# Residuals and the norms' scale and shift in natural rows on VectorE, and the front of a conditioned transformer block as two streams, each shifted by itself

## The chip, the cores and the metric

The kernel runs on one core of a Trainium2 chip. A core has five engines with an instruction queue each: TensorE (PE, matmuls into PSUM), VectorE (DVE), ScalarE (ACT), GpSimd (POOL) and SyncE (SP, which here only issues DMAs). They meet through semaphores alone. The metric is the device time of one launch in microseconds (us); less is better.

## What is computed

For each of 32 samples b (256 rows of 256 numbers), cut to what matters:

```python
x = rotate(x, theta[b], phi[b])                              # groups of 4 columns
h = gelu(x @ Wi[e] + bi[e])                                  # e = expert of the sample, 256 -> 1024
x = layernorm(h @ Wo[e] + bo[e] + x) * gamma[e] + beta[e]    # residual, norm 1
c = branch of the sample                                     # 0 or 1: two products; 2: three, through 512
x = layernorm(x + branch_c(x)) * gamma2 + beta2              # residual, norm 2
scale, shift = split(silu(sin_emb(t[b])) @ W_ada + b_ada)    # two rows of 256
x = layernorm(x) * (1 + scale) + shift                       # norm 3
q, k, v = x @ Wq + bq, x @ Wk + bk, x @ Wv + bv              # 16 heads of 16
s = q @ k.T / 4 + bias[b, head];  s[mask] = -inf
x = x + softmax(s) @ v @ Wo + bo                             # residual
x = x + gated_gelu((layernorm(x) * g2 + beta2) @ W1 + b1) @ W2 + b2
```

## The kernel before, in words

**Precision and layouts.** A product of width 256 takes its operand turned (columns on partitions). The products behind the first norm use operands split in a high and a low part (`xa_hi`, `xa_lo` for the branch, `xb_hi`, `xb_lo` for q, k and v, `xc_hi`, `xc_lo` in the tail): three matmuls for one. Norms work in natural rows (rows of the sample on partitions), so each norm's result is turned by TensorE (`transposed`, 128x128 pieces against `ident`), and ScalarE copies it out of PSUM.

**Scale and shift.** Before the change, norm 1 and norm 3 are scaled and shifted after the turn, when gamma and beta are numbers per partition: `affine_T` on ScalarE does two ACTIVATEs from PSUM into `gelu_out` and one more for the high part. VectorE then makes the low part.

**Residuals.** They are added by TensorE into the PSUM bank that collects the product. `open_wide` opens `SUM_F` with the bias row and adds x through eight matmul instructions of `x0` against `ident`; `add_residual` adds `xa_hi` and `xa_lo` in the branch, and `xb_hi` and `xb_lo` in the tail (bank `SUM_T`), through four matmuls each against `eye`. The bias row is picked by a 128x128 selector; for norm 1 and the branch ScalarE fills it anew for each sample (`stage_sel`). In the tail ScalarE copies `SUM_T` to `xo_nat` before VectorE takes its statistics.

**Three streams.** `front(b)` holds the rotation, the wide expert product (four steps m2 = 0 to 3 of `wide_in`, gelu on ScalarE, `wide_out`), norm 1, the branch, norms 2 and 3, and q, k, v. `attention(b)` holds 16 heads: on TensorE `scores` into `pS` and `turn` into `pX`, on VectorE bias, row maximum and subtraction (two times L1106, two times L913), on ScalarE the exponential. `tail(b)` holds the output product and the feed-forward part. Each is a generator, one step at a `yield`.

**What sets the order.** `ORDER` has a string per engine; each letter takes the next step of f (front), h (attention) or r (tail). One pass over the string is a turn; in turn n an engine goes through `front(n)`, `attention(n - 1)` and `tail(n - 2)`:

```python
streams = {"f": front(it) if it < NB else None,
           "h": attention(it - 1) if it else None,
           "r": tail(it - 2) if it >= 2 else None}
for letter in ORDER[engine]:
```

A turn begins with the wide product. Its four steps use PSUM banks 0 and 1 in turn (`BANK`), and the branch, q, k and v share the same two. An engine never overtakes itself: a waiting instruction holds all that stands behind it in its queue.

**Start.** In the first turn the weights are loaded in eleven pieces and split (`w_hi` on ScalarE, `w_lo` on VectorE); `weights()` hands out one portion per step. Pieces 6 to 10 reuse staging space of earlier ones, so SyncE's queue waits for their split. ScalarE's functions lie in table sets: Gelu in one, Exp and Tanh in another, and a change of set is an instruction of its own (ACT_TABLE_LOAD).

Of the kernel before, what the change touches and what calls it, by code (L numbers as in the profile page):

```python
# [7 lines left out]
P = 128  # L8
F32 = mybir.dt.float32
# [9 lines left out]
VECTORS = (("L2_cond_b1_sr", 4), ("L2_cond_b2_sr", 2), ("L3_cond_b_ada", 4), ("L3_cond_bq", 2), ("L3_cond_bk", 2),  # L19
# [20 lines left out]
    "PE": "ffffhfhhfhhhhfrfhhrrhhfhhfhrhhffhrfhhrhhrhhrhhhhrhhfrhhffhhhrhhhfrhhfh",  # L40
    "ACT": "ffhfhfhrhrhfhfhrfrhrhrrhhrhhhfhrfrfhrhhfhfh",
    "DVE": "hhhhrfhfhrfrhfrhhfrfhrrhfhfrhhfrhffhrrhfrhhfhrf",
    "POOL": "frff",
    "SP": "hhhffhfhhfhhhhhhhhffhffhffr",
}


BANK = {"wide0": 0, "wide1": 1, "wide2": 0, "wide3": 1, "y1": 0, "narrow": 0, "deep0": 0, "deep1": 1, "deep2": 0,
        "x2": 1, "x0": 0, "q": 1, "k": 0, "v": 1}
# [4 lines left out]
    "dma_angles", "dma_ints", "dma_consts", "dma_idx", "dma_sels", "dma_rows", "dma_cols", "dma_bcast", "dma_ada",  # L54
# [4 lines left out]
    "dma_x", "dma_chosen", "dma_mask", "dma_out", "dma_spill", "dma_raw0", "dma_raw1", "dma_raw2", "dma_raw3", "dma_stack0",  # L59
    "dma_stack1", "dma_bias0", "dma_bias1", "dma_bias2", "dma_bias3",  # L60

    "dve_front", "x0_made", "x0_turned", "x0_copied", "sel_made", "wide_in", "wide_gelu", "wide_out",
    "y1_made", "y1_turned", "x1_aff", "x1_hi", "x1_lo", "pe_narrow", "act_narrow", "dve_narrow", "pe_deep", "act_deep",
    "dve_deep", "branch_done", "y2_scaled", "x2_made", "x2_turned", "x2_aff", "x2_hi", "x2_lo", "qkv", "qk_hi", "qk_lo",
# [4 lines left out]
    "dve_tail", "ctxT", "ctx_hi", "ctx_lo", "wo", "xo_made", "ffn_in_made", "ffn_turned", "x3_aff", "x3_hi", "x3_lo",  # L69
    "w1", "tanh", "gated", "ffn_hi", "ffn_lo", "w2", "out_made",  # L70

    "front_var", "front_eps", "front_rstd", "tail_var", "tail_eps", "tail_rstd")
# [10 lines left out]
def conditioned_stack(nc, x_in, fside_in, mask_in, a, out_d):  # L83
# [14 lines left out]
    with ctx:  # L98
# [6 lines left out]
        eye = sb("eye", [P, P], F32R)  # L105
# [36 lines left out]
        xb = [(sb(f"xb_hi{i}", [P, K, S], F32R), sb(f"xb_lo{i}", [P, K, S], F32R)) for i in range(2)]  # L142
# [3 lines left out]
        xo_nat = sb("xo_nat", [P, T, H])  # L146
        ffn_in = sb("ffn_in", [P, T, H])
        gamma2 = sb("gamma2", [P, H])
# [4 lines left out]
        chosen = sb("chosen", [P, 2, M + 2 * K + K])  # L153
        mod = sb("mod", [P, 2 * K, NB])
# [7 lines left out]
        bias_raw = xo_nat[0:NROWS, 0, :]  # L162

        bias_rows = sb("bias_rows", [P, H], F32R)
        select = sb("select", [R2, 2, NB])
        stage_sel = sb("stage_sel", [P, 2, P], F32R)

        sels = sb("sels", [P, 3 * P + NM], F32R)
        o_sel, ff_sel, v_sel = (sels[:, n * P:(n + 1) * P] for n in range(3))
        hid_sel = sels[:, 3 * P:3 * P + NM]  # L170
        zero_sel = sb("zero_sel", [P, P], F32R)
        ones = sb("ones", [R2, P])
        idx = sb("idx", [1, 3, NB], I32)
        stats, mean_var, var_eps, rstd = ({which: sb(f"{which}_{name}", [P, T] + size) for which in ("front", "tail")}
# [11 lines left out]
        q_spill = nc.dram_tensor("q_spill", (2, 2, 3, HD * NPAIR * S), F32, kind="Internal").ap()  # L186
        k_spill = nc.dram_tensor("k_spill", (2, 2, 3, HD * NPAIR * S), F32, kind="Internal").ap()
# [4 lines left out]
        sels_raw = flat(ctx_nat[:, :, :])[:, 3 * NB:3 * NB + 3 * P + NM]  # L192
# [3 lines left out]
        trig = xo_nat[:, 1, 0:6 * NB].rearrange("p (q n) -> p q n", q=2)  # L196
        emb_act = scratch[:, 9 * NB:11 * NB].rearrange("p (q n) -> p q n", q=2)
        ada = gated[:, :, :, :].rearrange("p a b c -> p (a b c)").rearrange("p (k n) -> p k n", k=K)
# [36 lines left out]
        def interleave(engine, front, attention, tail, weights=None):  # L235

            extra = weights() if weights else iter(())
            for it in range(NB + 2):
                streams = {"f": front(it) if it < NB else None,
                           "h": attention(it - 1) if it else None,  # L240
                           "r": tail(it - 2) if it >= 2 else None}
                for letter in ORDER[engine]:
                    if streams[letter] is not None:
                        next(extra, None)
                        next(streams[letter], None)
                assert all(s is None or next(s, "end") == "end" for s in streams.values())


        def sync_program(e):
# [19 lines left out]
            def load_chosen(b):  # L269

                if b >= 2:
                    e.wait_ge(sem["branch_done"], b - 1)
                n = M + 2 * K
                load(chosen[:, b % 2, 0:n], a["expert_cols"].rearrange("e p n -> p e n")
                     [:, bass.ds(chosen_expert[b], 1), :].rearrange("p a n -> p (a n)"), "dma_chosen")
                c = e.value_load(idx[0:1, 1, b:b + 1], min_val=0, max_val=2)
                load(chosen[:, b % 2, n:n + K], a["branch_cols"].rearrange("e p n -> p e n")
                     [:, bass.ds(c, 1), :].rearrange("p a n -> p (a n)"), "dma_chosen")

            def load_x(b):  # L280
                if b:
                    e.wait_ge(sem["x0_turned"], b)
                load(flat(x_nat[:, :, :]), x_in[b], "dma_x")
# [22 lines left out]
            fetch_expert(0, 3)  # L306

            def weights():
# [12 lines left out]
                load_x(1)  # L321
# [8 lines left out]
                for u in range(NBIAS):  # L330
                    load_bias(u)
                yield

            def front(b):
# [6 lines left out]
                if b + 2 < NB:  # L341
                    load_x(b + 2)
# [947 lines left out]
```

## Time and profile before

| | us |
|---|---|
| median of three runs (range) | 2272.45 (2271.24 to 2272.83) |
| the profiled execution, its own time | 2269.38 |
| its span, first to last instruction | 2267.6 |
| busy PE / DVE / ACT / POOL | 2071.2 / 1456.6 / 1213.6 / 141.5 |
| mean granted TensorE clock | 0.981 |

Busy time is a union of instructions on an engine. Matmuls overlap in the pipeline, so what one costs in a dense stretch is the distance from its start to the next start. Of the 32 samples, 10 take the branch with three products (52 high parts of branch activations are made: one for a sample of the short branches, three for one of the long).

### The profile page before, as it was taken

What the parts mean: (1) busy time and instruction counts of PE and PEld (TensorE: products, weight loads), DVE (VectorE), ACT (ScalarE), POOL (GpSimd) and SP (SyncE); (2) the same over time, 40 slices, a digit from 0 to 9 for tenths busy, and PEclk for the clock granted to TensorE, in tenths of its full rate; (3) what the DMA queues carried; (4) which work ended last, traced back from release to release, by engine and by line L of the source; (5) the groups of instructions that cost most, each with busy time, mean ns of one, the idle gap of its engine ahead of it and who ended that gap; (6) DMA issues with size and microseconds to landing.
All of it is one profiled execution on the core that took longest, in us unless ns stands there. A gap on an engine that the chain in (4) does not pass through costs nothing.

```text
span 2267.6 us, 44771 instructions
## 1 busy us (share of the span) xinstructions
PE 2071.2 (91%) x15545; PEld 1823.4 (80%) x15545; DVE 1456.6 (64%) x5093; ACT 1213.6 (54%) x2151; POOL 141.5 (6%) x269
## 2 busy tenths in 40 slices
PE   5789999999999999999999999999999999999976
PEld 4678888888888888888888878888888888888865
DVE  4456776666676566676666776666676666677653
ACT  3455555555555655555555555555555565555532
POOL 1000000000000000000000000000000000000000
PEclk8889999999999999999999999999999999999988
DMA  5554445555444554444554445554545555444440
GB/s 197 160 152 135 151 123 163 165 159 147 138 144 142 160 160 138 153 144 140 164 169 128 136 142 155 164 169 141 151 140 138 164 165 157 140 146 125 121 129 24
DMA packets 208341, 330.98 MB, mean 146 GB/s; under 512 B 27970, under 2 KB 114402, under 8 KB 208098
## 3 DMA queue, kind: packets, MB, share of 16 engines
q1 hardware_dynamic: 208098, 327.79, 49.2%
q8 instruction: 147, 2.41, 0.4%
q14 instruction: 96, 0.79, 0.1%
HBM read 268.99 MB, written 58.72 MB: 145 GB/s over the span
## 4 chain that ended last, share of the span: by engine, by line
PE 76%; DVE 14%; issue 5%; ACT 3%; DMA 0%; POOL 0%; SPq 0%; DVEq 0%; POOLq 0%; ACTq 0%
PE pD L388 48%; PE pX L614 10%; PE pS L388 9%; PE pC L388 6%; DVE x_scores L1106 4%; DVE x_scores L913 3%; PE pD L393 3%; DVE x_nat L910 2%; PE pC L634 1%; ACT L713 1%; DVE y_nat L910 1%; ACT gated L713 1%; DVE gated L916 1%; DVE y_nat L1002 1%; ACT probs L713 1%
## 5 line engine op out<-in xcount | busy, mean ns | idle before, releaser
L1106 DVE CUSTOM_DVE_ANT_0 x_scores<-pS,bias_ring 128x256 f32<-128x256 f32 x1024 | 391.5, 419 | 410.0 <-PE pS L388 407.6
L713 ACT ACTIVATE probs<-pX 128x512 f32<-128x512 f32 x512 | 305.1, 596 | 471.5 <-PE pX L614 469.2
L614 PE MATMUL pX<-ident,x_scores 128*128 128x128 f32 x2048 | 327.2, 283 | 107.5 <-DVE x_scores L913 69.5
L614 PEld LDWEIGHTS pX<-ident,x_scores 128*128 128x128 f32 x2048 | 226.1, 142 | 177.1 <-DVE x_scores L913 106.1
L913 DVE TENSOR_SCALAR x_scores<-x_scores,row_max 128x256 f32<-128x256 f32 x1024 | 315.5, 350 | 18.3
L388 PE MATMUL pS<-k_stack,q_stack 96*128 96x256 f32 x1024 | 304.7, 380 | 0.0
L713 ACT ACT_TABLE_LOAD x188 | 241.2, 1283 | 25.7 <-DVE xa_lo L910 21.9
L388 PE MATMUL pD<-raw,gelu_out 128*128 128x256 f32 x1024 | 241.8, 379 | 0.0
L388 PE MATMUL pD<-x,raw 128*128 128x256 f32 x1024 | 239.2, 382 | 1.0 <-ACT x L713 0.8
L388 PEld LDWEIGHTS pS<-k_stack,q_stack 96*128 96x128 f32 x1024 | 197.9, 193 | 22.3
L388 PEld LDWEIGHTS pD<-x,raw 128*128 128x128 f32 x1024 | 191.3, 192 | 25.5 <-issue 1.6
L388 PE MATMUL pD<-w_hi,ffn 128*128 128x256 f32 x1024 | 210.1, 288 | 0.6 <-ACT ffn L713 0.6
L388 PE MATMUL pS<-mask_add,eye_bf 128*128 128x512 bf16 x512 | 196.0, 383 | 10.6 <-issue 8.6
L388 PEld LDWEIGHTS pD<-raw,gelu_out 128*128 128x128 f32 x1024 | 184.9, 190 | 20.2
L713 ACT ACTIVATE gelu_out<-pD,chosen 128x256 f32<-128x256 f32 x364 | 158.1, 486 | 50.5 <-PE pD L388 36.2
L388 PEld LDWEIGHTS pD<-w_hi,ffn 128*128 128x128 f32 x1024 | 167.8, 191 | 14.0 <-issue 12.3
L713 ACT ACTIVATE gated<-pD 128x512 f32<-128x512 f32 x128 | 75.9, 593 | 149.1 <-PE pD L388 149.1
L1191 POOL TENSOR_SCALAR front_var_eps<-front_mean_var 128x2 f32<-128x2 f32 x96 | 29.7, 309 | 1860.9 <-DVE front_mean_var L995 1860.9
L388 PE MATMUL pC<-probs,v_aug 128*17 128x256 f32 x2048 | 139.4, 391 | 0.7 <-issue 0.7
L388 PE MATMUL pD<-xc_hi,w_hi 128*128 128x256 f32 x512 | 129.1, 284 | 0.0
L388 PE MATMUL pD<-xc_hi,w_lo 128*128 128x256 f32 x512 | 129.0, 284 | 0.0
L388 PE MATMUL pD<-w_lo,ffn 128*128 128x256 f32 x512 | 127.8, 282 | 0.0
(155 smaller groups left out, 3795.6 us busy)
## 6 DMA issues: line engine op xcount, KB each, us to landing
bias_ring<-in_fside SPq DMA_DIRECT2D x512, 256.0 KB, 2.7
raw<-in_experts SPq DMA_DIRECT2D x128, 512.0 KB, 4.3
q_spill<-hid SPq DMA_DIRECT2D x96, 256.0 KB, 3.2
k_spill<-hid SPq DMA_DIRECT2D x96, 256.0 KB, 2.6
q_stack<-q_spill SPq DMA_DIRECT2D x128, 192.0 KB, 4.9
k_stack<-k_spill SPq DMA_DIRECT2D x64, 384.0 KB, 6.0
x_nat<-in_x SPq DMA_DIRECT2D x32, 256.0 KB, 3.0
out<-xo_nat SPq DMA_DIRECT2D x32, 256.0 KB, 7.0
```

Of the source, the lines that this page charges most:

```text
L388: return e.matmul(o, lhsT, rhs, start=start, stop=stop, skip_group_check=True, **kw)
L393: last = e.transpose(pD[:, bank, k, t * P:(t + 1) * P], src_nat[:, t, k * P:(k + 1) * P], ident[:, :])
L614: last = e.transpose(pX[:, k, t * P:(t + 1) * P], x_scores[:, u % NX, t, k * P:(k + 1) * P], ident[:, :])
L634: last = e.transpose(pC[:, 1, t * P:(t + 1) * P], ctx_raw[:, t * P:(t + 1) * P], ident[:, :])
L713: return e.activation(o, i, func, bias=bias, scale=scale)
L910: return e.tensor_tensor(o, a, c, op)
L913: return e.tensor_scalar(o, a, s1, None, op0) if op1 is None else e.tensor_scalar(o, a, s1, s2, op0, op1)
L916: return e.scalar_tensor_tensor(o, a, s, c, op0, op1)
L1002: last = e.tensor_scalar(dst[:, t, :], srcs[t], mean_var[which][:, t, 0:1], rstd[which][:, t:t + 1], ALU.subtract, ALU.mult)
L1106: e.tensor_tensor_reduce(x_scores[:, xn, t, :], pS[:, t, :], bias_ring[:, n, t, :], 1.0, -3.4e38, ALU.add, ALU.max, row_max[:, xn, t:t + 1 ...
L1191: e.tensor_scalar(var_eps[which][:, :], mean_var[which][:, :, 1], eps, 1.0, ALU.add, ALU.mult).then_inc(sem[which + "_eps"], 1)
```

## The change

**Residuals.** TensorE's residual matmuls and the tail's copy to `xo_nat` are gone. The rows that are to be added are kept in natural form (`x_nat`, `y_nat`, and a new `res` with three buffers), and `summed` on VectorE adds the PSUM bank to them before the statistics.

**Scale and shift.** `scaled` on VectorE applies them in natural rows, for norms 1 and 3 with gamma and beta as rows on all partitions (`norm1`, `norm3`), which DMAs bring per sample. `norm3` comes from `mod_rows`, a table of all samples that the kernel itself makes at the start, writes to DRAM and reads back. ScalarE makes only the high part, straight from PSUM, and VectorE the low part from PSUM.

**Selectors.** One column is read as if it were 128 (`select`, `sels`, with `to_broadcast`), so ScalarE fills none.

**Streams.** The front is split: `wide(b)` (letter g: turn x, the wide product, norm 1) and `front(b)` (the rest). The wide product has PSUM bank 0 for itself (`WIDE`), and each of its steps now waits for the gelu of the step before it; the branch has banks 0 and 1, and q, k and v all use bank 1. A table `SKIP` says how many letters of f, h and r an engine skips at the start, so each stream is shifted by steps and not by whole turns. On TensorE, `SKIP` of (2, 56, 27) puts the wide product of a sample beside heads 9 to 15 of the attention of two samples earlier.

```diff
 ORDER = {
-    "PE": "ffffhfhhfhhhhfrfhhrrhhfhhfhrhhffhrfhhrhhrhhrhhhhrhhfrhhffhhhrhhhfrhhfh",
+    "PE": "gfhghhrghhghhfghhghhhhgghhghhrrhhhfhhhfrfrhhrfhhfhrhhrhhhrhhrrhhfrhfhh",
...
+SKIP = {"PE": (2, 56, 27), "ACT": (4, 33, 28), "DVE": (5, 31, 32), "POOL": (0, 0, 2), "SP": (3, 20, 3)}
...
+WIDE, BANK = 0, {"y1": 1, "narrow": 0, "deep0": 0, "deep1": 1, "deep2": 0, "x2": 1, "q": 1, "k": 1, "v": 1}
```

On SyncE, at the end of `weights()`, and the two loads per sample:

```diff
+            def load_norm1(b):
+                if b:
+                    e.wait_ge(sem["y1_made"], b)
+                load(flat(norm1[:, :, :]), a["expert_rows"][bass.ds(chosen_expert[b], 1), :].rearrange("a n -> (a n)")
+                     .partition_broadcast(P), "dma_norm1")
+
+            def load_norm3(b):
+                if b:
+                    e.wait_ge(sem["x2_made"], b)
+                load(flat(norm3[:, :, :]), mod_rows[b].partition_broadcast(P), "dma_norm3")
...
+                e.wait_ge(sem["dve_mod"], 1)
+                load(mod_rows, mod_made, "dma_mod")
+                e.wait_ge(sem["dma_mod"], 16)
+                load_norm3(0)
```

On VectorE:

```diff
+            def summed(srcs, bank, which, name, n):
+
+                for t in range(T):
+                    tt(srcs[t], pD[:, bank, t, :], srcs[t], ALU.add).then_inc(sem[name], 1)
+                for t in range(T):
+                    e.wait_ge(sem[name], T * n + t + 1)
+                    last = e.bn_stats(stats[which][:, t, :], srcs[t])
+                step(last, "dve_" + which)
...
+            def scaled(srcs, dst, which, n, gamma, beta, scaled_, made_):
+
+                e.wait_ge(sem[which + "_var"], n + 1)
+                for t in range(T):
+                    last = stt(dst[t], srcs[t], mean_var[which][:, t, 0:1], gamma, ALU.subtract, ALU.mult)
+                step(last, scaled_)
+                e.wait_ge(sem[which + "_rstd"], n + 1)
+                for t in range(T):
+                    last = stt(dst[t], dst[t], rstd[which][:, t:t + 1], beta, ALU.mult, ALU.add)
+                step(last, made_)
```

**TensorE, the tail's residual.** The rows are TensorE's at the output product of the tail. `bias_rows,sels` opens the sum, `eye,xb_hi` and `eye,xb_lo` are the residual, `w_hi,xc_hi` is where the product begins. Before:

```order
L388 MATMUL pS<-k_stack,q_stack 128x256 x2
L388 MATMUL pD<-bias_rows,sels 128x512
L388 MATMUL pD<-eye,xb_hi 128x128 x4
L388 MATMUL pD<-eye,xb_lo 128x128 x4
L388 MATMUL pD<-w_hi,xc_hi 128x256
L388 MATMUL pD<-w_lo,xc_hi 128x256
```

After the change:

```order
L425 MATMUL pD<-bias_rows,select 128x512
L425 MATMUL pD<-bias_rows,sels 128x512
L640 MATMUL pX<-ident,x_scores 128x128 x4
L425 MATMUL pS<-mask_add,eye_bf 128x512
L425 MATMUL pS<-k_stack,q_stack 128x256 x2
L425 MATMUL pD<-w_hi,xc_hi 128x256
L425 MATMUL pD<-w_lo,xc_hi 128x256
```

The eight residual matmuls are gone, and a head's work stands between the opening and the product.

**ScalarE, the wide product's gelus among the exponentials** (`gelu_out<-pD,chosen` is a gelu, `probs<-pX` the exponential of a head). Before:

```order
L713 ACT_TABLE_LOAD
L713 ACTIVATE gelu_out<-pD,chosen 128x256 x4
L713 ACT_TABLE_LOAD
L713 ACTIVATE probs<-pX 128x512
L713 ACT_TABLE_LOAD
L713 ACTIVATE gelu_out<-pD,chosen 128x256 x2
L713 ACTIVATE ctx_raw<-pC 128x256
L713 ACTIVATE gelu_out<-pD,chosen 128x256 x2
L713 ACT_TABLE_LOAD
L713 ACTIVATE probs<-pX 128x512
```

After the change, from the first gelu of a sample to the third:

```order
L737 ACT_TABLE_LOAD
L737 ACTIVATE gelu_out<-pD,chosen 128x256 x2
L737 ACTIVATE gated<-pD 128x512
L737 ACT_TABLE_LOAD
L737 ACTIVATE probs<-pX 128x512
L737 ACT_TABLE_LOAD
L737 ACTIVATE gelu_out<-pD,chosen 128x256 x2
L737 ACT_TABLE_LOAD
L737 ACTIVATE probs<-pX 128x512 x2
L737 ACT_TABLE_LOAD
L737 ACTIVATE gelu_out<-pD,chosen 128x256 x2
```

The four steps of a sample's wide product had two changes to the gelu set, and now have four. In the branch the exponential of a head now stands between its first gelu step and the place of the third product's, where there were none.

**SyncE, the end of the weights' loading at the start.** The rows after the change; `x_scores<-in_weights` is the last piece of the weights, `mod_rows` the table for norm 3:

```order
L267 DMA x_scores<-in_weights 128x512 [waits dve_w]
L267 DMA x_nat<-in_x 128x512 [waits y1_scaled]
L267 ISA [waits y1_made]
L267 DMA norm<-in_expert_rows 128x512
L267 DMA bias_ring<-in_fside 128x512 [waits dve_w]
L267 DMA bias_ring<-in_fside 128x512 x3
L267 DMA mod_rows<-ctx_nat 32x512 [waits dve_mod]
L267 DMA norm<-mod_rows 128x512 [waits dma_mod]
L267 DMA q_spill<-hid 128x2x256 [waits qk_lo]
```

Before the change the same place held the last piece, a load of x and four loads of the bias, and then the spill of q; the write and the read of `mod_rows` and the load of `norm1` are new.

## Rows read from the trace of the kernel before

**Rows 1.** The page's busy times: us (share of the span) x instructions.

```profile
PE 2071.2 (91%) x15545; PEld 1823.4 (80%) x15545; DVE 1456.6 (64%) x5093; ACT 1213.6 (54%) x2151; POOL 141.5 (6%) x269
```

**Rows 2.** Busy time in a stretch of full turns: us (x instructions), granted clock, DMA.

```profile
1000.00:1500.00 500.00, 471.33 (x3614) 417.08 (x3613) 333.66 (x1171) 278.92 (x499) 31.10 (x58) 1.00 0.50 149
```

**Rows 3.** TensorE's waits, 300 to 2000 us: total, times, longest.

```profile
PE pX L614 <- DVE x_scores L913: 43.1, 51, 1.1
PE pX L614 <- ACT probs L713: 28.1, 25, 1.2
PE pD L393 <- DVE x_nat L910: 16.6, 25, 0.7
```

**Rows 4.** Timeline, TensorE: the turning of x in two neighbouring turns (start, us).

```profile
466.63 0.66 PE L393 MATMUL pD<-ident,x_nat 128*128 128x128 f32 x4 [0.66 <-DVE x_nat L910]
...
533.13 0.66 PE L393 MATMUL pD<-ident,x_nat 128*128 128x128 f32 x4 [0.66 <-DVE x_nat L910]
```

**Rows 5.** Timeline, TensorE: the residuals of x and of the tail, with neighbours.

```profile
1025.06 0.58 PE L388 MATMUL pD<-bias_rows,stage_sel 128*128 128x512 f32 x1
1025.48 1.05 PE L388 MATMUL pD<-ident,x 128*128 128x128 f32 x8
1026.37 1.89 PE L388 MATMUL pD<-raw,gelu_out 128*128 128x256 f32 x8
...
1041.68 0.40 PE L388 MATMUL pD<-bias_rows,sels 128*128 128x512 f32 x1
1041.92 0.56 PE L388 MATMUL pD<-eye,xb_hi 128*128 128x128 f32 x4
...
1042.76 0.34 PE L388 MATMUL pD<-w_hi,xc_hi 128*128 128x256 f32 x1
```

**Rows 6.** Groups by line and form, ScalarE: busy us, mean ns, idle before.

```profile
L713 ACT ACT_TABLE_LOAD x188 | 241.2, 1283 | 25.7 <-DVE xa_lo L910 21.9 <-PEq L1281 0.7 <-issue 0.4
```

**Rows 7.** Timeline, ScalarE, around a change of table set.

```profile
1022.03 0.60 ACT L713 ACTIVATE probs<-pX 128x512 f32<-128x512 f32 x1
1022.65 1.28 ACT L713 ACT_TABLE_LOAD   x1
1023.94 0.84 ACT L713 ACTIVATE gelu_out<-pD,chosen 128x256 f32<-128x256 f32 x2
```

**Rows 8.** Groups by line and form, VectorE: a head's work, a norm's passes, an addition.

```profile
L1106 DVE CUSTOM_DVE_ANT_0 x_scores<-pS,bias_ring 128x256 f32<-128x256 f32 x1024 | 391.5, 419 | 410.0 <-PE pS L388 407.6 <-issue 0.6 <-DVE y_nat L916 0.5
L913 DVE TENSOR_SCALAR x_scores<-x_scores,row_max 128x256 f32<-128x256 f32 x1024 | 315.5, 350 | 18.3
L1002 DVE TENSOR_SCALAR y_nat<-pD,front_mean_var,front_rstd 128x256 f32<-128x256 f32 x64 | 31.7, 537 | 1.2 <-POOL front_rstd L1194 1.2
L916 DVE SCALAR_TENSOR_TENSOR y_nat<-y_nat,front_rstd,beta 128x256 f32<-128x256 f32 x64 | 28.2, 482 | 1.4 <-POOL front_rstd L1194 0.3
L910 DVE TENSOR_TENSOR y_nat<-x_nat,rot_sin 128x256 f32<-128x256 f32 x64 | 24.3, 422 | 0.0
```

**Rows 9.** Timeline, VectorE, first turn: norm 3 of sample 0, the next weight piece.

```profile
57.08 0.73 DVE L1002 TENSOR_SCALAR y_nat<-y_nat,front_mean_var,front_rstd 128x256 f32<-128x256 f32 x2 [0.86 <-POOL front_rstd L1194]
61.68 1.22 DVE L916 SCALAR_TENSOR_TENSOR w_lo<-x_scores,w_hi 128x1024 fp32r<-128x1024 f32 x1 [3.87 <-ACT w_hi L713]
```

**Rows 10.** Timeline, SyncE's queue, first turn: the last weight piece, the bias loads.

```profile
56.25 0.33 SPq L251 DMA_DIRECT2D x_scores<-in_weights  x1
...
66.61 2.59 SPq L251 DMA_DIRECT2D bias_ring<-in_fside  x4
```

**Rows 11.** DMA issues: KB each, median us to landing; a store, a load to all partitions.

```profile
q_spill<-hid SPq DMA_DIRECT2D x96, 256.0 KB, 3.2
...
gamma<-in_gamma SPq DMA_DIRECT2D x1, 128.0 KB, 5.0
```

**Rows 12.** Timeline, TensorE: the scores of two heads in the first attention.

```profile
85.58 0.38 PE L388 MATMUL pS<-mask_add,eye_bf 128*128 128x512 bf16 x1
...
88.22 0.38 PE L388 MATMUL pS<-mask_add,eye_bf 128*128 128x512 bf16 x1
```

**Rows 13.** TensorE's waits, 2140 us to the end: total, times, longest.

```profile
PE pS L388 <- issue: 7.7, 1, 7.7
```

More of the change, by code:

```diff
@@ L233, in uses, with interleave, over @@
             return sum(1 for j in range(i + 1) if stage(j) == stage(i))
[L235 removed]
+        def interleave(engine, wide, front, attention, tail, weights=None):
             extra = weights() if weights else iter(())
[L238 to L241, printed above, removed]
+            def over(stream, n, extra):
+                for b in range(n):
+                    for _ in stream(b):
+                        if not b:
+                            next(extra, None)
+                        yield
+            streams = {"g": over(wide, NB, extra), "f": over(front, NB, extra),
+                       "h": over(attention, NB + 1, iter(())), "r": over(tail, NB, iter(()))}
+            skip = dict(zip("fhr", SKIP[engine]))
+            next(extra, None)
+            for _ in range(NB + 4):
                 for letter in ORDER[engine]:
[L243 to L244 removed]
+                    if skip.get(letter):
+                        skip[letter] -= 1
+                    else:
                         next(streams[letter], None)
[L246 removed]
+            assert all(next(stream, "end") == "end" for stream in streams.values())
         def sync_program(e):
@@ L378, in tail @@
                 e.wait_ge(sem["out_made"], b + 1)
-                load(out_d[b].rearrange("(t p) h -> p t h", p=P), xo_nat[:, :, :], "dma_out")
+                load(out_d[b].rearrange("(t p) h -> p t h", p=P), res[:, b % 3, :, :], "dma_out")
                 yield
-            interleave("SP", front, attention, tail, weights)
+            interleave("SP", wide, front, attention, tail, weights)
             e.wait_ge(sem["dma_out"], 16 * NB)
@@ L706, in tail @@
                     yield
-            interleave("PE", front, attention, tail, weights)
+            interleave("PE", wide, front, attention, tail, weights)
         def scalar_program(e):
@@ L895, in tail @@
                     yield
-            interleave("ACT", front, attention, tail, weights)
+            interleave("ACT", wide, front, attention, tail, weights)
         def vector_program(e):
@@ L1138, in tail @@
                 yield
-                rows = [xo_nat[:, t, :] for t in range(T)]
-                e.wait_ge(sem["xo_made"], b + 1)
-                statistics(rows, "tail")
+                rows = [res[:, b % 3, t, :] for t in range(T)]
+                e.wait_ge(sem["wo"], b + 1)
+                summed(rows, SUM_T, "tail", "dve_xo", b)
                 yield
@@ L1207, in tail @@
                 yield
-            interleave("POOL", front, attention, tail)
+            interleave("POOL", wide, front, attention, tail)
         block = ctx.enter_context(nc.Block())
```

378 lines of the change are left out of this document (179 added, 199 removed).

## The prediction, as it was made before the changed kernel ran

> **What bounds the kernel now.** I read the busy times first. TensorE is busy 2071.2 of 2267.6 us, VectorE 64% and ScalarE 54% [rows 1]. In full turns TensorE's share is higher still, 471.3 of 500 us at a granted clock of 1.00, beside 333.7 us of VectorE and 278.9 us of ScalarE [rows 2]. So TensorE bounds, and the next question is what it waits for: in 1700 us of full turns the head's turning waits 43.1 us for VectorE's subtraction and 28.1 us for the exponential of the head before, and the turning of x waits 16.6 us for the rotation [rows 3]. A turn with a short branch lasts 533.13 - 466.63 = 66.5 us [rows 4], so 1700 us are 25.6 turns and these waits make 3.4 us of a turn. The reader should see two things: a matmul that goes away is worth nearly all of its distance to the next start, and TensorE waits on two neighbours that the change loads differently.
>
> **What TensorE loses.** Distances between starts [rows 5]: the residual of x costs 1026.37 - 1025.48 = 0.89 us. Its opening takes 1025.48 - 1025.06 = 0.42 us, the tail's opening 1041.92 - 1041.68 = 0.24 us; I take it that the new opening costs what the tail's does, 0.18 us less. The tail's residual costs 1042.76 - 1041.92 = 0.84 us. The branch's residual is the same eight matmuls, again 0.84 us. Together 2.75 us a sample. The first and last samples stand where TensorE waits for others anyway, so I count 31: **-85 us**. A selector read as one repeated column is not in the trace: its bound from below is no cost, from above one more opening as dear as the dearest, 0.18 us three times a sample (17 us); I take none, since it takes the same place in the same instruction, and keep 17 us for the range.
>
> **What VectorE gains.** Six additions of 128x256 per sample. The nearest row is 24.3 / 64 = 0.38 us each; a pass with three inputs is 28.2 / 64 = 0.44 us [rows 8]; so 192 of them are 73 us, 84 us at the most. Norms 1 and 3 take four passes where two were: for norm 1 56 us instead of 31.7, for norm 3, whose two old passes I price as additions, 56 instead of 24 [rows 8]. Together about 130 us, 4.1 us a sample: VectorE goes from 1457 to about 1585 us. That is no bound by share (44.3 us of a turn from rows 2, then 48 of 64). But it is not spread evenly. By the order, from the last `wide_out` of a sample to its q, VectorE has 9 heads at (391.5 + 315.5) / 512 = 1.38 us [rows 8], three sums with statistics, three scaled norms, ten passes of 128x512 and small ones: 12.4 + 5.3 + 5.3 + 6.9 + 3 = 33 us, priced by rows 8 (a 512 pass as two additions or a little less). TensorE has in the same stretch about 31 to 32 us: its turn of 62.6 us (0.943 of 66.5 [rows 2]) less 2.75, less what stands outside (k, v, the four wide steps, seven heads: 28 us). The two are equally long there, and each head passes from one to the other. So the waits for the subtraction don't go away. The rotation gets ten more us of lead over the turning of x, so I strike that wait (0.65 us of a turn) and add the same and a little more to the other two: 3.6 us instead of 3.4, **+6 us**. The bounds are 1.2 us (only the surplus of VectorE's 33 us in that stretch, -75 us) and 6 us (+75 us).
>
> **What ScalarE gains and loses.** It loses four passes of norms 1 and 3, two selectors and a copy of `xo_nat`, work beside TensorE's in any case, and worth nothing by itself. It gains changes of table set. By the order a sample has eight in the wide product instead of four, and three or four in the branch instead of two: 11 or 12 where 188 / 32 = 6 were [rows 6]. With the first and last samples about 350 instead of 188, at 1.283 us: +205 us, more than it loses. The block load, two gelus, load, exponential lasts 1.28 + 0.84 + 1.28 + 0.60 = 4.0 us [rows 7]. A head on TensorE gets 64 / 16 = 4.0 us. The exponential of head h must be done before head h + 1 is turned, and in the wide stretch TensorE has, by the order and the distances of rows 5, a `wide_in` or `wide_out` (1.7 us), sometimes v or values too, between two turnings. I followed the blocks step by step with these durations: each `wide_in` finds its gelu done by 0.5 to 2 us, though it now waits for the gelu just before it. I cost the changes of set at nothing; their cover is those wide steps, and without it each block would show up to 1.3 us. In the branch the exponentials of two heads stand behind a load that even a short branch does; that is in the 3.6 us.
>
> A change of set is where the Trainium skill speaks against this change. Row 7's load starts 0.02 us behind the exponential and the gelu 0.01 us behind the load, so here a change costs its 1.28 us and no more [rows 7]. The page "ScalarE: Activation LUTs", section What ACT_TABLE_LOAD costs, adds 1.38 us of drain to each, 2.66 us in all. By that the 160 changes would cost ScalarE some 425 us, the block would be 6.8 us long, and TensorE would wait in every one of them; by the trace the block is as long as a head.
>
> **Start.** Norm 3 of sample 0 now waits for `norm3`. It stands behind the write and read of `mod_rows`, and those in SyncE's queue behind the last weight piece, issued at 56.25 us, two more loads and the four bias loads (2.59 us) [rows 10]. So the write goes at about 60.5 us, lands 3.2 us later as a store does, and the read lands 5.0 us after that at the latest as a load to all partitions does [rows 11], 3 us at the best: 66.7 to 68.7 us, where before the norm's pass began at 57.08 us [rows 9]. Behind it stand the low part of x, the rotation of sample 1 and its turning. Ten us late; 3.9 us come back, since VectorE stood still there for a weight piece [rows 9]. So +6, and four steps of the wide product of sample 1 (7 us) now stand ahead of the first scores: about +12 us.
>
> **End.** Those four steps and the rest of a wide product (13.7 us) are missing in the other half of the last attention but one. Seven heads alone can't go faster than the first ones went, 88.22 - 85.58 = 2.64 us each [rows 12]; with k and v beside them TensorE loses some 5 us there, so 8.5 us are gained. The 7.7 us in which the last attention's first scores stood still behind their own spill [rows 13] have three heads more of lead, of which I count half: together -12 us. Start and end make **0 us**.
>
> **The sum.** Against the profiled execution's own time: 2269.4 - 85 + 6 + 0 = 2190 us. The median of the runs before stands 3 us above that execution, so **2193 us**, 3.5% less.
>
> **The rivals.**
>
> A. The forecast, 2193 us, with its own range of 2165 to 2225 (waits 1 us a turn less or more): 0.64.
>
> B. VectorE becomes the bound between `wide_out` and q. For it: 33 us against 31 to 32. Against it: it is idle in the other half of a turn, and order could shift. At 1.4 us more waiting a turn, 2193 + 31 x 1.4 = 2236 us: 0.14.
>
> C. The shift by steps takes the waits away. For it: three of the four things that TensorE waited for got another place. Against it: the stretch above. With 1.8 us of waits left, 2193 - 31 x 1.8 = 2137 us: 0.13.
>
> D. Slower than before. Place: the five more blocks of load, gelus, load in a turn. Price: with half of the 205 us on TensorE's path, 2193 + 100 = 2293 us. It decides from 79 / 31 / 5 = 0.5 us per block on. Against it: TensorE waits 1.1 us of a turn for the exponential now, in one place, where two changes and five gelu passes stand between two exponentials. The rule "group by table-set" of the same page of the Trainium skill (Rules for kernel authors) says this is how it must go. 0.07.
>
> E. The freed time is only waited away, 2270 us: 0.02. The residual matmuls are on a queue that is busy 94%, which speaks against it.
>
> **Numbers.** Below 2130 us neither bound of the waits reaches but with every other term at its best; above 2245 us lie D, E and the worst of B. The range of 2130 to 2245 leaves out some 2 in 10. Faster by over 0.2% (about what this kernel's runs can tell from no change) are A, B and C, 0.91; within 0.2% most of E, 0.02; slower D, 0.07.
>
> **What the changed profile would show.** A turn with a short branch of 63 to 64 us. TensorE busy about 1980 us, VectorE 1585, ScalarE 1310, with about 350 table loads at the same 1283 ns. No wait for x in full turns, but waits of the head's turning for the subtraction, most of them between the turning of y1 and q. The first scores at about 94 us. I would be wrong if the turning of heads 9 to 15 waits for exponentials (D), if `wide_in` waits for `gelu_out`, if VectorE has no idle time from the first sum to the low part of x (B), or if the additions from PSUM take over 0.5 us.

## The result, and the profile after

Over four executions each, before took 2271.84 us (2268.20 to 2272.83) and the changed kernel **2252.78 us** (2250.72 to 2254.92): a ratio of 0.9919, 95% interval 0.9902 to 0.9936. It is faster, by 0.8% and not by the 3.5% forecast, and outside the range of 2130 to 2245 us. The profiled execution took 2250.72 us.

The busy times of the page, then the group of table loads, and the page's shares of the chain that ended last:

```profile
PE 2024.3 (90%) x14735; PEld 1739.7 (77%) x14735; DVE 1563.6 (70%) x5410; ACT 1314.8 (58%) x2086; POOL 122.6 (5%) x268
...
PE 62%; DVE 11%; DMA 9%; SPq 6%; issue 6%; ACT 5%; DVEq 0%; ACTq 0%; POOL 0%; POOLq 0%
PE pD L425 41%; DMA out<-res 8%; PE pX L640 8%; PE pS L425 7%; SPq L267 5%; DVE x_scores L1131 3%; PE pC L425 3%; PE pD L430 2%; ACT gelu_out L737 2%; DVE x_scores L917 2%; DVE res L920 2%; ACT hid L737 1%; PE pC L660 1%; DVE res L914 1%; DVE xc_lo L914 1%
...
L737 ACT ACT_TABLE_LOAD x347 | 445.2, 1283 | 34.7 <-PE pD L425 28.1
```

Beside [rows 1] and [rows 6] this is, for two engines and the loads, what was forecast: 347 loads (about 350) at the same 1283 ns, ScalarE 1315 us (1310), VectorE 1564 (1585). TensorE is not: it is busy 2024 us where I had about 1980, so only half of the time that it was to lose is gone. The new thing is in the chain: 8% of it is a DMA, the store of a finished result (`out<-res`). It was in no term of the sum.

TensorE's waits in full turns, 300 to 2000 us (total, times, longest), to be read beside [rows 3]:

```profile
PE pD L430 <- DVE res L920: 32.7, 25, 2.6
PE pX L640 <- DVE x_scores L917: 24.2, 40, 1.3
PE pD L425 <- ACT hid L737: 16.3, 8, 2.0
PE pD L425 <- ACT xc_hi L737: 14.4, 49, 0.3
PE pD L425 <- DVE gated L920: 12.8, 26, 0.6
PE pD L425 <- issue: 3.3, 14, 0.4
```

The waits for x and for exponentials are gone, and the one for the subtraction has nearly halved. In their place stands one of 1.3 us a turn for `res`, which is norm 3's output ahead of the turning of x2; one of 2.0 us in every turn whose branch is long (`hid`); and two short ones of the tail.

The chain in one full turn, from where the store is issued; start, us, what:

```profile
455.36 0.43 SPq L267
455.83 0.43 SPq L267
...
457.86 6.93 DMA out<-res
464.79 0.77 issue
...
465.97 0.49 DVE res L920
466.52 0.37 issue
466.88 0.49 DVE res L920
467.42 0.66 PE pD L430 x4
```

The rows of x2 go into `res[:, b % 3]`, and the line ahead of norm 3's passes is `e.wait_ge(sem["dma_out"], 16 * (b - 2))`: the buffer has to be stored first. SyncE's queue in the same place shows why that is late (start, us):

```profile
453.34 0.35 SPq L267 DMA_DIRECT2D raw<-in_experts  x1
...
456.44 1.37 SPq L267 DMA_DIRECT2D raw<-in_experts  x3
457.86 0.81 SPq L267 DMA_DIRECT2D out<-res  x1
```

And the DMA issues of the whole run: KB each, median us to landing.

```profile
x_nat<-in_x SPq DMA_DIRECT2D x32, 256.0 KB, 7.6
...
out<-res SPq DMA_DIRECT2D x32, 256.0 KB, 7.6
```

The store stands behind the four loads of 512 KB of expert weights and needs 7.6 us to land. The prediction's only price for a store was the spill of q, 3.2 us for the same size [rows 11]. The store of the result itself was already slow in the kernel before, and none of TensorE's waits in full turns was for it:

```profile
out<-xo_nat SPq DMA_DIRECT2D x32, 256.0 KB, 7.0
```

**Where the time went.** From one turning of x to the next, 30 times: before 65.09 to 2091.87 us, 67.56 us a turn; after 84.59 to 2073.47 us, 66.30. So the turns gave 38 us. The first of these turnings came 19.5 us later, and the stretch behind the last is as long as it was (175.5 against 175.7 us). 38 - 19.5 = 18.5 us is, to 0.2 us, the difference of the two spans (2267.6 - 2248.9 = 18.7).

### The profile page after: what moved, and what is told of

The parts are those of the page before. It is cut to its first block, busy times and chain, and to the rows that moved or that the text cites. A ratio compares the mean times of both kernels' runs of the same rounds, so it can differ in the third digit from the quotient of the medians.

```text
span 2248.9 us, 43734 instructions
## 1 busy us (share of the span) xinstructions
PE 2024.3 (90%) x14735; PEld 1739.7 (77%) x14735; DVE 1563.6 (70%) x5410; ACT 1314.8 (58%) x2086; POOL 122.6 (5%) x268
## 4 chain that ended last, share of the span: by engine, by line
PE 62%; DVE 11%; DMA 9%; SPq 6%; issue 6%; ACT 5%; DVEq 0%; ACTq 0%; POOL 0%; POOLq 0%
PE pD L425 41%; DMA out<-res 8%; PE pX L640 8%; PE pS L425 7%; SPq L267 5%; DVE x_scores L1131 3%; PE pC L425 3%; PE pD L430 2%; ACT gelu_out L737 2%; DVE x_scores L917 2%; DVE res L920 2%; ACT hid L737 1%; PE pC L660 1%; DVE res L914 1%; DVE xc_lo L914 1%
## 5 line engine op out<-in xcount | busy, mean ns | idle before, releaser
L737 ACT ACT_TABLE_LOAD x347 | 445.2, 1283 | 34.7 <-PE pD L425 28.1
L640 PEld LDWEIGHTS pX<-ident,x_scores 128*128 128x128 f32 x2048 | 237.7, 143 | 129.6 <-DVE x_scores L917 97.8
L425 PE MATMUL pD<-x,raw 128*128 128x256 f32 x1024 | 244.0, 381 | 3.6 <-ACT gelu_out L737 2.9
L425 PEld LDWEIGHTS pD<-raw,gelu_out 128*128 128x128 f32 x1024 | 189.9, 190 | 23.5
L425 PEld LDWEIGHTS pD<-x,raw 128*128 128x128 f32 x1024 | 186.3, 191 | 25.6 <-issue 5.1
L1147 DVE RECIPROCAL rden<-pC 128x8 f32<-128x8 f32 x128 | 26.0, 203 | 185.1 <-PE pC L660 185.1
L737 ACT ACTIVATE gelu_out<-pD,chosen 128x256 f32<-128x256 f32 x300 | 125.8, 470 | 37.5 <-PE pD L425 36.1
L737 ACT ACTIVATE hid<-pD,cols 128x256 fp32r<-128x256 f32 x128 | 53.6, 469 | 136.5 <-PE pD L425 136.5
```

The costliest lines, as they stand in the source:

```text
L425: return e.matmul(o, lhsT, rhs, start=start, stop=stop, skip_group_check=True, **kw)
L640: last = e.transpose(pX[:, k, t * P:(t + 1) * P], x_scores[:, u % NX, t, k * P:(k + 1) * P], ident[:, :])
L737: return e.activation(o, i, func, bias=bias, scale=scale)
L1147: step(e.reciprocal(rden[:, :, :], v[:, :, :, HD]), "rden_made")
```

## The experiments

Ratios are to the kernel before on the same chip. The kernel before was run again beside each group of experiments, and its median moved between 2266.7 and 2272.9 us; where two kernels of different groups are compared, the ratios are safer than the times. Theory Q says that norm 3 waits for the buffer, whose store is late in SyncE's queue; theory V, the rival, that VectorE's own work (my rival B) is the bound.

### The store ahead of the expert weights

```diff
-    "SP": "fhhfhhhhhhhgfgggrhghhhhfhhf",
+    "SP": "fhhfhhhhhrhhgfggghghhhhfhhf",
```

> The changed kernel with one letter moved: SyncE stores a sample's result before it issues the next sample's four expert loads, not behind them. Theory Q (the queue): norm 3 writes into a buffer that the store must have left, and the store lands 7 us after its issue behind 2 MB of expert weights; TensorE's wait for the turning of x2 (1.3 us in each of 25 turns) goes, so about 30 us less, 2223 us, and VectorE's waits before norm 3 vanish. Theory V (VectorE is full between the last wide_out and q, and would be as late without the store): the wait changes its name only, under 8 us less, 2245 us or more.

**2207.36 us**, ratio 0.9704 (0.9683 to 0.9724): 45 us less, more than I expected. Its waits in the same 1700 us:

```profile
PE pX L640 <- DVE x_scores L917: 24.7, 42, 1.3
PE pD L425 <- ACT hid L737: 16.3, 8, 2.0
PE pD L425 <- ACT xc_hi L737: 14.8, 50, 0.3
PE pD L425 <- DVE gated L920: 12.9, 26, 0.6
```

SyncE's queue, where the store now goes out 8 us before the first expert load:

```profile
448.53 0.43 SPq L267 DMA_DIRECT2D out<-res  x1
...
456.49 0.35 SPq L267 DMA_DIRECT2D raw<-in_experts  x1
```

The wait for `res` is gone and nothing has come in its place. A turn now takes 64.84 us, and every short turn in the middle of the run 63.1 to 63.5, where it had scattered from 63.9 to 67.1. VectorE's work is unchanged (1561.6 us). Theory Q holds, V falls. That the early store has only thinned out the transfers at this point is a rival of Q; it is tested further below.

### Norm 3's table ahead of the last weight pieces

```diff
                     for i in pieces:
+                        if i == 10:
+                            e.wait_ge(sem["dve_mod"], 1)
+                            load(mod_rows, mod_made, "dma_mod")
+                            e.wait_ge(sem["dma_mod"], 16)
+                            load_norm3(0)
                         piece(i)
```

(and the same four lines taken out behind the four bias loads)

> The changed kernel, with the write and read of the table for norm 3 issued before the last weight piece and the bias loads, not behind them. Theory S (the start is late by this queue alone): TensorE's wait of 20.8 us for the first x2 falls below 10 us, and the kernel takes 10 to 12 us less, 2242 us. Rival: the first turn is held by the weight pieces anyway, and under 4 us are gained.

**2245.20 us**, ratio 0.9873 (0.9852 to 0.9894), 7.6 us less. The first wait for `res` shrinks from 20.8 to 8.4 us, and the first turning of x comes 10.3 us earlier; the turns are 0.17 us longer (66.47 us), since TensorE waits a little more for the store (36.2 instead of 32.7 us).

### The kernel before without its residual products

The `mm(...)` of x's residual and both `add_residual` are taken out and nothing put in their place.

> The kernel before, without its residual matmuls (x, the branch's and the tail's residuals are left out of the computation, nothing takes their place; all else and its order stay). If a matmul that goes is worth its distance to the next start, 2.6 us a sample go: 31 x 2.6 = 80 us less, 2191 us. If the order around them turns the freed time into waits for VectorE and ScalarE, about half: 2230 us. The first says that the sum's largest term was right and the loss lies in what the change adds; the second that the term itself was too large.

**2226.32 us**, ratio 0.9796 (0.9771 to 0.982), 46.6 us less. Waits from 300 to 2000 us:

```profile
PE pX L610 <- DVE x_scores L908: 42.6, 52, 1.1
PE pX L610 <- ACT probs L708: 28.1, 26, 1.2
PE pD L393 <- DVE x_nat L905: 17.3, 26, 0.7
PE pD L388 <- ACT xc_hi L708: 10.4, 18, 0.9
PE pS L388 <- issue: 8.7, 11, 2.6
```

By the distances of [rows 5] TensorE loses 2.6 us a turn, and a turn gets about 1.5 (short) or 2.3 us (long) shorter. These turns are of the profiled execution, which took 2216.75 us and is the fastest of four; the median is 9.6 us above it. The three old waits stay to the microsecond, and two new ones take 19 us. So this part alone is worth little more than half of what its matmuls weigh.

### One table for exponential and activation

```diff
-                        act(gelu_out[:, g, n, :], pD[:, bank, n, :], ACT.Gelu, bias=biases[n]).then_inc(sem[name], 1)
+                        act(gelu_out[:, g, n, :], pD[:, bank, n, :], ACT.Tanh, bias=biases[n]).then_inc(sem[name], 1)
```

This and the other activation, that of the wide product, in the changed kernel:

> The changed kernel with Tanh in place of Gelu (another function is computed), so that ScalarE needs no change of table set after the start: 345 loads of 1.28 us fewer. Theory L (loads matter only where one stands between a product of the long branch and its gelu, ten times 1.3 us with a fall of the granted clock behind each): 20 to 35 us less, 2225 us, and the clock's falls in full turns go. Rival D of the prediction (the loads are on the path in the wide product too): 60 us less or more. If loads are covered everywhere: 2250 us.

**2252.43 us**, ratio 0.9912 (0.989 to 0.9935): nothing, though ScalarE is busy 865 instead of 1315 us. The wait for `hid` falls from 16.3 to 6.1 us and that for `res` rises from 32.7 to 47.1: TensorE arrives earlier and waits longer for the same store. While one wait ends at a transfer that nothing moves, what is saved ahead of it can't be seen. So the question was put again with the store out of the way.

### Both early moves, and three kernels on top of them

> Two moves in SyncE's queue at once: the result of sample b - 3 is stored ahead of the expert weights (alone it gave 2207 us), and norm 3's table is fetched for sample 0 ahead of the last pieces of the weights (alone it gave 2245 us, 7.6 less than the changed kernel). If the two waits are separate, one at each turn's x2 turning and one at the start, the gains add up: 2207.4 - 7.6 = 2199.8, some 2195 to 2203 us. Theory S (what one ends, the other would have hidden: the start's gain is given back by the transfers of the first turns, since the result's early store had put the table's load 3.4 us later): 2205 to 2210 us.

**2193.87 us**, ratio 0.9669 (0.9651 to 0.9688). The moves add up: by the ratios 0.9704 - (0.9919 - 0.9873) = 0.9658, where the bracket is what the start's move gave alone. The 6 us below the forecast are mostly the runs' own level, since the kernel before stood 4 us lower beside this one. From x's turning at 75.39 to the one at 2017.04 us lie 30 turns of 64.72 us.

The same with Tanh for Gelu:

> The two moves of the run beside it, with Tanh in Gelu's place at both places, so that exponentials and activation share one table and ScalarE loads none in the turns. It computes another activation; all else is the same. Alone in the changed kernel this was worth nothing (2252.4 against 2252.8), while the first pass of norm 3 waited for the result's store. Theory L (only the ten turns of the long branch wait for a load, 2.0 us at the third product, and each wait is followed by a stretch at a lower clock of about 3.4 us, which costs 1.7): 10 x (1.2 to 2.9) us less than the run beside it, 12 to 30, so 2170 to 2188 us. Theory D (my rival of the table loads: 160 more loads on the path for much of their 1283 ns): 60 us or more off, 2140 or less. Theory N (loads are hidden everywhere): within 4 us of the run beside it.

**2179.62 us**, ratio 0.9604 (0.9587 to 0.9621), 14.3 us less. Short turns stay at 63.1 us, long ones go from 68.1 to 66.8.

The same with Gelu, and this ahead of the wait in the long branch:

```diff
+                    act(spare[:, :], minus_half[:, 0:1], ACT.Gelu)
                     e.wait_ge(sem["dve_deep"], 3 * b + 1)
                     deep(2)
```

> The two moves, and in the ten turns of the long branch a Gelu over one column of a constant on ScalarE ahead of its wait for the third product's first half, so that the table is in place when the product comes. It computes the same. Under theory L above the wait of 2.0 us shrinks by about 1.2 and the lower clock behind it goes with some of them: 12 to 25 us less than with the two moves alone, 2175 to 2188 us. Under theory N nothing, 2195 to 2203. If the load and its column push ScalarE's rows behind it later instead, slower than with the two moves alone by up to 10 us.

**2179.40 us**, ratio 0.9605 (0.9585 to 0.9624), 14.5 us less; none of the kernels here is faster beyond the noise. First the changed kernel, then this one: ScalarE's timeline around the third product's activation.

```profile
715.41 1.28 ACT L737 ACT_TABLE_LOAD   x1 [2.81 <-PE pD L425]
716.70 0.84 ACT L737 ACTIVATE gelu_out<-pD,cols 128x256 f32<-128x256 f32 x2
```

```profile
689.78 1.28 ACT L739 ACT_TABLE_LOAD   x1
691.08 0.20 ACT L739 ACTIVATE spare<-minus_half 128x1 f32<-128x1 f32 x1
692.58 0.84 ACT L739 ACTIVATE gelu_out<-pD,cols 128x256 f32<-128x256 f32 x2 [1.30 <-PE pD L427]
```

In the changed kernel ScalarE waits 2.81 us for the product and only then loads the table, with TensorE waiting behind it. Here the load runs during that wait, and TensorE waits 0.8 us instead of 2.0. Ten loads placed otherwise give as much as leaving all of them out (a turn is 64.31 us here and 64.22 with Tanh): the other 330 or so cost nothing that these runs can tell.

The two moves with norm 3's scale and shift left out:

> The two moves, with norm 3's multiplication by its scale and addition of its shift left out: the rows are normalized only, so the sums and the rows of x2 are others (the table is still loaded). VectorE has two passes of a sample's rows fewer ahead of x2's turning, some 1.6 to 1.8 us a sample. Theory V (VectorE's passes are on the path between the residual and x2's turning: my prediction's term for it was + 0.2 us a turn, its bounds 0 to 1): if the whole of the two passes is on the path, 32 x 1.7 = 54 us less than with the two moves alone; by my term some 6; if wide steps of TensorE hide it all, within 4 us. I take 6 to 20 us less.

**2181.62 us**, ratio 0.9612 (0.9595 to 0.9629), 12.3 us less than with the two moves alone; a short turn is 62.7 instead of 63.1 us. The 1.7 us a sample of the expectation is wrong: `scaled` takes four instructions of 0.48 us over the two tiles of the rows, and the normalization left here still takes two of 0.41. VectorE is busy 1531.6 instead of 1561.3 us, 0.93 us a sample less. So all of it on the path would have given 30 us, and 12.3 came: some 0.4 of these 0.93 us are exposed.

### Was it the buffer, or the crowd of transfers?

> The changed kernel with a fourth buffer of result rows, and SyncE's order left as it was: the store still goes out behind the expert weights and the four loads at 457.86 us of the turn, and still takes 7 us to land. The room comes from the rotation, which writes its products to the next sample's buffer in place of one of its own; its wait for the store is a turn older. If it is the buffer that norm 3 waits for (theory Q), the wait for res goes and the time is that of the kernel with the early store: 2207 us, some 2200 to 2215. If it is the crowd of transfers at that point, which the early store had thinned out (theory C), the wait for norm 3's table or for x's rows takes its place and the time stays above 2235. If rotation now waits for the store instead, 3 us behind its landing, it shows as a wait of VectorE with x_nat behind it.

```diff
-        res = sb("res", [P, 3, T, H])
+        res = sb("res", [P, 4, T, H])
...
             def rotate(b):
...
+                if b >= 4:
+                    e.wait_ge(sem["dma_out"], 16 * (b - 3))
...
-                if b >= 3:
-                    e.wait_ge(sem["dma_out"], 16 * (b - 2))
```

(The cut leaves out the buffer numbers and the rotation's tile `crossed`, whose place the fourth buffer takes. The last addition of a sample reads another sample's rows in this kernel, so it computes another sum with as many instructions.)

**2209.22 us**, ratio 0.9731 (0.9704 to 0.9759), with the early store 0.9704 (0.9683 to 0.9724): the intervals overlap. A turn is 64.71 us long, with both early moves 64.72. The store still takes as long, by the median of all of them in this kernel:

```profile
out<-res SPq DMA_DIRECT2D x32, 256.0 KB, 7.9
```

but nobody waits for it: neither TensorE's turning of x2 nor VectorE's rotation. The same with the two other edits:

> Four buffers of result rows again with SyncE's order of heads and stores as in the changed kernel, this time together with norm 3's table fetched early and the Gelu column ahead of the long branch's wait. The kernel with the early store and these two gave 2179.4. If it is only the buffer that norm 3 waited for, this one gives the same: 2175 to 2186 us. If the crowd of transfers costs something once the buffer is free, 5 us more or above. (In the run with four buffers alone, the second operand of the last addition of each sample was left at another sample's buffer, so its result was another sum, by as many instructions; here it is the sample's own.)

**2180.88 us**, ratio 0.9616 (0.9588 to 0.9644), against 0.9605 with three buffers and the early store; a turn is 64.31 us in both. So it is the buffer. The crowd of transfers costs nothing in these turns once nothing waits for the store.

### The kernel before with one table, and with both parts out

> The kernel before with Tanh in Gelu's place at both places (another activation is computed): 188 table loads less about ten. In the changed kernel with both early moves that was worth 14 us, 1.3 in each of nine turns of the long branch and 3 in the start. If the exposed load in the long branch came with the change (theory new), the long turns here stay at 70.2 us and the time within 8 us of 2272. If it was there before (theory old), the long turns fall by 1.3 and the time is 12 to 20 us less, 2252 to 2260. Since the long turns were 3.9 us above the short ones before and 5.0 with the change and the early moves, I expect the first.

**2228.66 us**, ratio 0.9818 (0.9778 to 0.9858): 41 us less. Neither of the two theories had that: the long turns fall by 1.1 us and the short ones by 1.5 (66.4 to 64.9). Its waits:

```profile
PE pX L614 <- DVE x_scores L913: 42.8, 52, 1.1
PE pD L393 <- DVE x_nat L910: 17.2, 26, 0.7
PE pD L388 <- issue: 8.0, 18, 0.6
```

The 28.1 us for exponentials of [rows 3] are gone. That wait was a table load. In the kernel before, ScalarE's timeline:

```profile
1060.10 1.28 ACT L713 ACT_TABLE_LOAD   x1
1061.39 0.60 ACT L713 ACTIVATE probs<-pX 128x512 f32<-128x512 f32 x1
```

and TensorE's, the turning that waits for that exponential:

```profile
1062.13 0.63 PE L614 MATMUL pX<-ident,x_scores 128*128 128x128 f32 x4 [0.98 <-ACT probs L713]
```

> The kernel before without its residual products (not computed) and with Tanh for Gelu. The first alone gave 46 us of the 83 that TensorE loses, the second 41 to 43. Theory A (two separate shares of the turn): they add up, 2272 - 46 - 42 = 2184 us. Theory I (the half of the residual's gain that was missing went into waits for exponentials behind a table load): more than the sum, 2272 - 83 - 30 or so, 2150 to 2170. Theory V (with both gone VectorE's subtractions are the next bound, 43 us of waits in either): less than the sum, 2195 to 2205. I take A, with V next, since the waits for exponentials stood at 28 us with and without the residual.

**2183.28 us**, ratio 0.9625 (0.959 to 0.9659). The kernel before stood 5 us lower beside it, so theory A is held against the product of the two ratios, 0.9796 x 0.9818 = 0.9618, and not against 2184 us. The two shares add up; theory V's 2195 us, a ratio of 0.966, lies just outside.

What the residuals weigh on TensorE is seen in this pair. The rows are as in [rows 2]: the stretch, its length, then TensorE's busy time and instructions. The stretch is the same 24 full turns each time, from the fifth turning of x to the 29th, first with the residuals, then without:

```profile
260.01:1852.82 1592.81, 1525.69 (x11664) 1350.25 (x11665) 1072.03 (x3785) 716.51 (x1465) 104.04 (x192) 1.00 0.53 153
255.88:1816.03 1560.15, 1474.02 (x11088) 1286.99 (x11089) 1071.95 (x3785) 718.71 (x1465) 104.13 (x192) 1.00 0.53 156
```

576 matmuls fewer are 2.15 us of a turn and not the 2.57 of their distances, and 0.8 us of that comes back as time in which TensorE is idle (2.8 and 3.6 us a turn). A turn is 1.36 us shorter.

## Why the prediction was wrong

By the profiled execution I had 2190 us and it took 2250.7. The turns account for 38 of these 60 us (1.26 us gained where -85 + 6 is 2.55 a turn), the 31st turn's share for 2.5, start and end for 20 (19.5 where I had 0).

1. **The step that failed** is "3.6 us instead of 3.4", + 6 us: it holds no wait for a transfer. I priced waits on engines alone, and put down the norm's passes without asking what the buffer that they write was waiting for. The largest wait of the changed kernel, 32.7 us in 1700 or 1.3 a turn, is for the store. With the store early the time is 2207 us and with a fourth buffer 2209, both inside my range. The size of the term hides this. TensorE's waits came to 3.9 us a turn (100.4 us in 25.6 turns), not far from 3.6; but with both early moves the waits for engines are 2.7 (71.5 us in 26.3 turns), so I had these too high and the store at nothing. The removal gave 45 us: behind the start the store's waits make 36.6 us in the whole run (28 waits of 57.4 us in all, less the 20.8 of the first), and most of the rest is TensorE's clock, of whose short falls fewer are left (below).

2. **The start.** I had + 12 us, it was + 19.5 at the first turning of x, and the first scores came at 105.0 us where I had 94. The step was the right one, the sizes were not. The write of `mod_rows` was issued at 61.12 us (I had 60.5), but the read behind it only at 67.06, 5.9 us later where I took a store's 3.2. With the table fetched early, 8.4 of the 20.8 us stay; what holds them was not tried.

3. **The end.** I had - 12 us, it was 0. The wait of 7.7 us [rows 13] did go, and the part up to the last turning of x2 is 4.7 us shorter with both moves (57.7 instead of 62.5). But the part behind it is 4 us longer (117.3 instead of 113.3). There the last heads run alone, and TensorE waits 16.3 us for the subtraction where it waited 8.6. This is read from the traces; no run tried it.

4. **TensorE's 2.75 us** a turn, my largest term, did not hold. These are the same 24 turns of the kernel before, the changed kernel, the one with four buffers, and the one with both moves and the load ahead:

```profile
263.76:1888.71 1624.95, 1530.76 (x11664) 1352.55 (x11665) 1074.17 (x3785) 906.06 (x1609) 102.39 (x192) 1.00 0.51 150
275.62:1871.65 1596.03, 1497.91 (x11068) 1293.78 (x11065) 1155.01 (x4026) 993.37 (x1569) 86.86 (x192) 0.99 0.53 160
276.30:1833.93 1557.63, 1488.01 (x11068) 1285.74 (x11065) 1152.53 (x4026) 993.35 (x1569) 87.05 (x192) 1.00 0.54 164
262.42:1808.04 1545.62, 1484.45 (x11068) 1281.28 (x11065) 1152.62 (x4026) 995.09 (x1577) 87.05 (x192) 1.00 0.55 165
```

A turn of them has 63.78 us of busy time before and 62.41 after, 1.37 us less; idle time went from 3.92 to 4.09. Some 0.4 of the missing 1.4 us go away with the store's waits and the falls of the clock behind them (62.00 with four buffers); the last kernel, at a granted clock of 1.00, has 61.85. So even there TensorE loses 1.9 us and not 2.75. The pair above says where a part of it went: without the residuals the neighbouring matmuls take 0.4 us a turn more. The rest, about 0.4 us, is in the other matmuls of the new order; what makes them dearer stays open. The turn with both moves is 2.84 us shorter than before all the same, since the new order takes 1.0 us of idle time away (3.92 to 2.90), the waits for x and for exponentials.

5. **The table loads (rival D)** were rightly costed at nothing in the wide product. Without the loads ScalarE is free for 450 us more (1314.8 against 864.4 us busy with both moves), and outside the long branches and the start TensorE gains nothing by it. Two places I had wrong. The ten long branches expose their load, 1.3 us each, since the wait for the product stands ahead of it; with 3 us of the start that is 14 us. And the wait for exponentials before, which I carried over into the new sum as part of 3.6 us, was a load that the new order covers. So the Trainium skill's "ScalarE: Activation LUTs", Rules for kernel authors (group by table-set), aims at something that was worth 41 us in the kernel before, with 188 loads, and no more than 14 in the changed one with 347. The 1.38 us of drain that the same page of the Trainium skill (What ACT_TABLE_LOAD costs) adds to a load is not in these traces: the load at 1060.10 us in the rows of the kernel before is followed by the next activation after 0.01 us.

6. **VectorE (rival B)** is not the bound: 45 us went while its work stayed. It came to + 107 us (I had + 130). It is not free either. Of the 0.93 us a sample that norm 3's scale and shift add, 0.4 us show in a turn; my sum had + 0.2 us a turn for all waits together.

That the kernel with both moves took 2193.87 us, where I had 2193, is luck in good part: its turns are 9 us better than my sum, its start and end 10 us worse, and within a turn TensorE loses 1 us less than I had while the waits for engines are nearly 1 us shorter. What was sound is that a matmul that goes frees time on a full engine, and that the loads in the wide product are covered. What was missing is one wait on a transfer.

## What to carry to other kernels

When a change gives a tile a new writer, list what else must be done with that buffer, down to the store that empties it, and find that store in the DMA queue: what stands ahead of it, and how long it takes in that company. Before's own DMA table can answer this while nobody waits yet. A table load costs what it delays: put it ahead of the wait with a small activation, and count exposed loads, not loads. And when an experiment gives nothing, look whether a wait elsewhere has grown by as much; take that wait away and ask again.

## What the runs showed of the hardware

TensorE's granted clock fell for about 3.4 us at a time, to its lower level (1.2 GHz), at nine places between 300 and 2000 us of the changed kernel, and at one in the kernel before. In these windows of the changed kernel (busy times, granted clock, DMA) it falls right behind the 2.04 us wait for `hid` at 718.25 us:

```profile
714.00:717.50 3.50, 2.21 (x19) 1.97 (x17) 0.44 (x3) 2.08 (x3) 0.88 (x2) 1.00 0.06 21
717.50:721.00 3.50, 2.68 (x15) 2.39 (x16) 2.73 (x10) 2.55 (x4) 0.00 (x0) 0.78 0.11 9
721.00:724.50 3.50, 3.50 (x29) 2.50 (x28) 2.83 (x13) 2.14 (x5) 0.88 (x2) 0.73 0.72 223
```

Five of the nine follow such a wait for `hid`, four a wait of 2.0 to 2.6 us for `res`; three other waits for `hid` of the same length have no fall behind them. The one fall before follows waits of 1.1 and 0.5 us. With both moves three such places are left, and none with both moves and the load ahead, where the waits for `hid` are 0.8 us. What a fall costs was not measured by itself. An estimate from the rows of the changed kernel and of the one with four buffers: nine falls and 1497.91 us of busy TensorE against three and 1488.01, the same instructions, so 1.65 us each.

A DMA's time to landing depends on what is issued with it. A 256 KB load of x took 3.0 us before and 7.6 after, of the same bytes, now issued behind the expert weights, norm 3's table and the store. With one letter of SyncE's order moved, the store of the result took 7.6 us behind the expert weights and 3.2 ahead of them.
